# The programs of TensorE, VectorE and ScalarE written out over the batch in fourteen stages of a transformer stack

## The reference

```python
x = _layernorm(x + _L0_attn_ref(x, ...))   # causal attention, 16 heads, rotary
x = _layernorm(x + _L0_ffn_ref(x, ...))    # two layers: local rotary attention, gated feed-forward
x = _layernorm(x + _L1_attn_ref(x, ...))   # attention with a table of relative biases
x = _layernorm(x + _L1_ffn_ref(x, ...))    # projection of values rounded to a 6 bit grid, scale per 32
x = _layernorm(x + _L2_attn_ref(x, ...))   # short convolution, then running sums over time
x = _layernorm(x + _L2_ffn_ref(x, ...))    # 16 routed and 2 shared experts
x = _layernorm(x + _L3_attn_ref(x, ...))   # linear recurrence in complex numbers
x = _layernorm(x + _L3_ffn_ref(x, ...))    # as in layer 0
```

```python
# L2: the scan
phi = k_val[..., None] * theta
num_re = cumsum(p_w * cos(phi), axis=1); num_im = cumsum(p_w * sin(phi), axis=1)
out_re = sum(s_re * qr + s_im * qi, axis=-1)
...
# L1: the quantised projection
q = nearest_on_grid(blocks / scales, GRID)
out = (xq * xs) @ (wq * ws).T + bias
```

## Time and profile before

| | |
|---|---|
| time, median of 3 runs | 7667.36 us (7658.31 to 7671.06) |
| profiled execution | 7661.74 us, its span 7660.0 us |
| granted TensorE clock, mean | 0.92 |
| TensorE products busy | 6397.9 us (84%) x31876 |
| TensorE weight loads busy | 3356.0 us (44%) x31876 |
| VectorE busy | 4648.5 us (61%) x11517 |
| ScalarE busy | 2779.5 us (36%) x6066 |
| GpSimd busy | 1304.2 us (17%) x1035 |

### The profile page before, as it was taken

How to read it: one execution, slowest core, us unless ns; L and a number is a source line. 1 busy time by engine, 2 the same in 40 slices (tenths; PEclk the granted TensorE clock), 3 DMA queues, 4 the chain that set the end, 5 groups by cost and what they waited for, 6 DMA issues and landing times. The chain is left out here.

```text
span 7660.0 us, 115272 instructions
## 1 busy us (share of the span) xinstructions
PE 6397.9 (84%) x31876; PEld 3356.0 (44%) x31876; DVE 4648.5 (61%) x11517; ACT 2779.5 (36%) x6066; POOL 1304.2 (17%) x1035
## 2 busy tenths in 40 slices
PE   6788868989998966999994387986996888998979
PEld 2333334655555533333332253334554455544655
DVE  5665467733864634888875747984335765347735
ACT  0255514712462200566661104541110255224711
POOL 1101115100610003000000003550002441015100
PEclk9899979989999987999997599997998899999999
DMA  5423244542455255332323221115222355324541
GB/s 177 117 67 70 54 148 153 175 143 73 138 184 169 76 213 188 81 80 71 85 57 106 80 80 56 37 32 143 67 64 74 126 163 183 99 87 151 178 150 54
DMA packets 931136, 851.29 MB, mean 111 GB/s; under 512 B 222216, under 2 KB 785376, under 8 KB 930464
## 3 DMA queue, kind: packets, MB, share of 16 engines
q1 hardware_dynamic: 500624, 522.99, 23.8%
q10 hardware_dynamic: 430080, 323.08, 13.2%
HBM read 503.10 MB, written 346.00 MB: 111 GB/s over the span
## 5 line engine op out<-in xcount | busy, mean ns | idle before, releaser
L1267 ACT ACTIVATE Catt_E<-Catt_t 128x512 f32<-128x512 f32 x1024 | 582.5, 596 | 345.8 <-DVE Catt_t L1230 164.0
L1216 DVE CUSTOM_DVE_ANT_0 Catt_S<-Catt_s,Catt_win 128x1024 f32<-128x1024 f32 x512 | 622.7, 1218 | 90.7 <-PE Catt_s L1139 62.1
L1216 DVE CUSTOM_DVE_ANT_0 Aatt_S<-Aatt_s,Aatt_win 128x128 f32<-128x128 f32 (+7 forms) x512 | 375.6, 757 | 251.4 <-PE Aatt_s L1139 239.8
L1267 ACT ACTIVATE Aatt_E<-Aatt_t 128x512 f32<-128x512 f32 (+3 forms) x768 | 355.2, 489 | 250.2 <-PE Aatt_t L1171 171.5
L1168 PE MATMUL Catt_t<-Catt_Q,Catt_K 123*128 123x512 bf16 x1024 | 369.3, 385 | 38.4 <-ACT Catt_E L1267 17.4
L1139 PE MATMUL Catt_s<-Catt_K,Catt_Q 96*128 96x512 bf16 x1024 | 321.2, 397 | 22.2 <-DMA Catt_K<-k_parts 12.1
L1194 PE MATMUL Catt_o<-Catt_E,Catt_V 128*32 128x256 f32 x4096 | 326.5, 391 | 0.0
L2358 PE MATMUL scan_cum<-scan_X,scan_upto 128*128 128x512 f32 x512 | 265.3, 608 | 25.3 <-DVE scan_X L2427 23.9
L1168 PE MATMUL Aatt_t<-Aatt_Q,Aatt_K 99*128 99x512 bf16 (+3 forms) x768 | 241.4, 333 | 51.9 <-ACT Aatt_E L1267 27.6
L2356 PE MATMUL scan_cum<-scan_X,scan_after 128*128 128x512 f32 x448 | 239.7, 617 | 44.0 <-DVE scan_pi L2438 44.0
L1230 DVE TENSOR_TENSOR Catt_t<-Catt_t,Catt_near 128x384 f32<-128x384 f32 (+1 forms) x384 | 200.4, 522 | 116.6 <-PE Catt_t L1168 112.9
(11 more groups left out here) (723 smaller groups left out, 14584.6 us busy)
## 6 DMA issues: line engine op xcount, KB each, us to landing
moe_cb<-c_s SPq DMA_DIRECT2D x16, 1024.0 KB
bias_rows<-line SPq DMA_DIRECT2D x16, 960.0 KB, 7.1
skewed<-bias_win ACTq DMA_DIRECT2D x16, 960.0 KB
Catt_win<-skewed SPq DMA_DIRECT2D x16, 960.0 KB, 5.0
rec<-state_in_r ACTq DMA_DIRECT2D x32, 416.0 KB
scan_r<-rec SPq DMA_DIRECT2D x64, 208.0 KB, 2.5
Aatt_Q<-q_parts SPq DMA_DIRECT2D x32, 384.0 KB, 4.4
Aatt_K<-k_parts SPq DMA_DIRECT2D x32, 384.0 KB, 5.6
```

The lines of the kernel that those rows point to most:

```text
L1216: v.tensor_tensor_reduce(out=S[:, j % 2, 0:w], in0=s_ps[j % 2][:, 0:w], in1=win[:, 0 if causal else h, w0:w0 + w], scale=-1.0, scalar=BIG, ...
L1267: a.activation(E[:, kb % NB, h, lo:hi], t_ps[n % 2][:, 0:hi - lo], ACT.Exp, scale=scale).then_inc(exped, 1)
```

## The change

Fourteen calls of `pipelined` become `written_out`, and eight `Fori` loops become Python loops, on TensorE, VectorE and ScalarE of nine stage functions: `stage_project` (Eout), `stage_qkv` (Aqkv, Cqkv), `stage_local_out` (B0, B1, H0, H1), `stage_thin_out` (Aout, Cout), `stage_qkv_rotary` (four), `stage_mx_project` (Dmx), `stage_state_inputs`, `stage_state_scan` and `stage_recurrence` (lru). In these stages the three engines' programs are then straight code over all four batches. The programs of SyncE and GpSimd are as before, as are the attention stages, the gated feed-forward, the experts, the bias tables and the first stage. No instruction that computes, moves or waits is added, taken away or reordered on its engine; register and branch instructions go, and waits are for constants.

The built program goes from 18,572 to 21,183 instructions on TensorE, from 13,899 to 17,942 on VectorE and from 10,085 to 11,250 on ScalarE, since a loop's body stood there once and now stands three or four times.

```diff
@@ -427,7 +427,7 @@
                     ins = t.matmul(tail.y[s][:], aT[:, s, k * P:(k + 1) * P], w_sb[:, k, :], start=k == 0, stop=k == F - 1)
                 ins.then_inc(tail.y_done, 1)
 
-            pipelined(t, B, NT, ((0, turn_in), (1, product), (LN + 1, lambda it, u: tail.turn(t, it, u))))
+            written_out(t, B, NT, ((0, turn_in), (1, product), (LN + 1, lambda it, u: tail.turn(t, it, u))))
 
         @block.scalar
         def _(s):
...
@@ -509,7 +509,7 @@
         def _(t):
             t.sem_inc(v_done, NT)
             t.wait_ge(w_in, nw)
-            with t.Fori(0, B) as it:
+            for it in range(B):
                 for c in range(2):
                     t.wait_ge(h_in[c], it * 16 + 16)
                     for j, (m, w) in enumerate(steps):
...
@@ -904,7 +904,7 @@
         @block.vector
         def _(v):
             v.sem_inc(z_done, NT)
-            with v.Fori(0, B) as it:
+            for it in range(B):
                 for u in range(NT):
                     c, q = u // 4, u % 4
                     if q == 0:
...
@@ -1356,17 +1356,17 @@
                                    start=k == 0, stop=k == KT - 1)
                 ins.then_inc(tail.y_done, 1)
 
-            pipelined(t, B, NT, ((0, product), (LN, lambda it, u: tail.turn(t, it, u))))
+            written_out(t, B, NT, ((0, product), (LN, lambda it, u: tail.turn(t, it, u))))
 
         @block.vector
         def _(v):
             tail.prime_dve(v)
-            pipelined(v, B, NT, ((0, lambda it, u: tail.combine(v, it, u)),))
+            written_out(v, B, NT, ((0, lambda it, u: tail.combine(v, it, u)),))
 
         @block.scalar
         def _(a):
             tail.prime_act(a)
-            pipelined(a, B, NT, ((LN, lambda it, u: tail.store(a, it, u)),))
+            written_out(a, B, NT, ((LN, lambda it, u: tail.store(a, it, u)),))
             tail.finish(a)
 
 
...
@@ -2051,7 +2051,7 @@
                 for u in range(c * 4, c * 4 + 4):
                     tail.combine(v, it, u)
 
-            pipelined(v, B, 2, ((0, quantise), (1, combine)))
+            written_out(v, B, 2, ((0, quantise), (1, combine)))
 
 
 K, KQ, SH, SM = 32, 4, 8, 8
...
@@ -2446,7 +2446,7 @@
                 v.tensor_tensor(y[:, j % 2, :].rearrange("p (k h) -> p k h", k=16), ys[j % 2][:, 0:P].rearrange("p (k h) -> p k h", k=16),
                                 r[:, j % R, 3 * P + 16:].unsqueeze(2).to_broadcast([P, 16, SH]), ALU.mult).then_inc(y_done, 1)
 
-            pipelined(v, B, ST, ((1, fraction), (0, phase), (2, weigh), (3, read), (4, reduce)))
+            written_out(v, B, ST, ((1, fraction), (0, phase), (2, weigh), (3, read), (4, reduce)))
 
 
 def stage_experts(nc, act_in, router, wg, wu, wd, c_s, out):
@@ -2897,12 +2897,12 @@
                 for u in range(c * 4, c * 4 + 4):
                     tail.turn(t, it, u)
 
-            pipelined(t, B, 2, ((0, inputs), (2, turn), (1, outputs)))
+            written_out(t, B, 2, ((0, inputs), (2, turn), (1, outputs)))
 
         @block.scalar
         def _(a):
             tail.prime_act(a)
-            with a.Fori(0, B) as it:
+            for it in range(B):
                 for u in range(NT):
                     tail.store(a, it, u)
             tail.finish(a)
...
```

More of the change, by code:

```diff
@@ L442, in move_in @@
                 s.activation(aT[:, sl, :], a_ps[sl][:], act).then_inc(aT_done, 1)
-            pipelined(s, B, NT, ((0, move_in), (LN + 1, lambda it, u: tail.store(s, it, u))))
+            written_out(s, B, NT, ((0, move_in), (LN + 1, lambda it, u: tail.store(s, it, u))))
             tail.finish(s)
@@ L450, in _ @@
             combine = lambda it, u: tail.combine(v, it, u)
-            pipelined(v, B, NT, ((0, combine),))
+            written_out(v, B, NT, ((0, combine),))
 def stage_qkv(nc, name, act_in, wq, wk, wv, wqs, wks, bias, rope, q_s, k_s, v_s, scale):
@@ L1607, in turn @@
                     ins.then_inc(turned, 1)
-            pipelined(t, B, NT, ((0, products), (LAG, turn)))
+            written_out(t, B, NT, ((0, products), (LAG, turn)))
         @block.scalar
@@ L1641, in turned_out @@
                                 qo[:, o, :].rearrange("p (j t) -> p j t", j=4)).then_inc(qo_out[o], 16)
-            pipelined(a, B, NT, ((0, squares), (0, values), (LAG, turned_out)))
+            written_out(a, B, NT, ((0, squares), (0, values), (LAG, turned_out)))
             for i in range(2):
@@ L2158, in running @@
                 t.matmul(d_ps[:], upto[:], pw[:, u, :], start=u == 0, stop=True, skip_group_check=True).then_inc(den_done, 1)
-            pipelined(t, B, NT, ((0, products), (1, running)))
+            written_out(t, B, NT, ((0, products), (1, running)))
         @block.vector
@@ L2229, in weights @@
                 v.drain()
-            pipelined(v, B, NT, ((0, scores), (1, weights)))
+            written_out(v, B, NT, ((0, scores), (1, weights)))
         @block.scalar
@@ L2257, in store @@
                             ).then_inc(rec_out[m % 2], 16)
-            pipelined(a, B, NT, ((0, decayed), (1, store)))
+            written_out(a, B, NT, ((0, decayed), (1, store)))
             for i in range(2):
@@ L2391, in store @@
                             y[:, m % 2, :]).then_inc(y_out[m % 2], 16)
-            pipelined(a, B, ST, ((1, trig), (0, whole), (4, store)))
+            written_out(a, B, ST, ((1, trig), (0, whole), (4, store)))
             for i in range(2):
@@ L2938, in combine @@
                     tail.combine(v, it, u)
-            pipelined(v, B, 2, ((0, states), (1, combine)))
+            written_out(v, B, 2, ((0, states), (1, combine)))
 def bass_post_layernorm_stack(nc, ins, out):
```

## The result

The changed kernel took 7642.7 us (median of 9 runs, 7634.4 to 7646.6) against 7668.0 us (9 runs, 7658.3 to 7682.0): ratio 0.9962, 95% interval 0.9953 to 0.9971, 25 us less. The prediction said 18.4 us less (7649.0, range 7634 to 7664). The profiled execution took 7643.5 us, its span 7641.8 us.

A forecast was written before the change was run, and what follows sets the result against it. The kernel was taken as a sum of stages behind barriers, each bound by its own engine. Gains of 24.0 us less 5.6 for fetch gaps gave 18.4, from 7667.4 to 7649.0 us, range 7634 to 7664.

The forecast's parts named there:

- The price of a loop pass on VectorE: Aout, Cout, Eout, Dmx, lru, scan: VectorE's loop entries, passes and returns go, 17.5 us gained, Aout 3.0, scan 3.7.
- The fetch gaps: VectorE's longer straight code: one idle gap per 128 instructions, 32 more, 16 on the path at 0.35, 5.6 us lost.
- What a return adds before that wait is hidden by the transfer. 0.25 each, 1.0: Local outs (B0, B1, H0, H1): TensorE's wait ends with a DMA landing, which hides the return; 1.0 us gained in all.
- The same kind of cycle, 0.5: State inputs: ScalarE waits for the record's store, and register time in that cycle goes; 0.5 us gained.
- 1.0 each for Aqkv and Cqkv: VectorE waits for its own stores; part of ScalarE's and VectorE's register time is in that cycle, 2.0 us gained together.
- ScalarE as the one waited for, 3.0: TensorE waits for ScalarE's copy L282; address computations between copies go, gaining 2 us in lru and 1 in Eout.
- Rotary 0: Rotary projections: TensorE is full and VectorE's register work lies beside it, so 0 us gained.
- Busy time of every engine is unchanged: Whole kernel: a sign expected in the profile after the change, every engine's busy time as before.
- rival A: Gain swallowed by waits in Eout, Dmx, Cout and lru, with TensorE partly at its low clock: 7657.6, chance 0.35.
- Wrong would be the sum if any stage gains over 6 us (C): Any stage: a gain over 6 us was to show that each loop return is a fetch from memory.
- Rival B: Slower: fetching the straight programs costs 20 stalls of 2.5 us on VectorE, ScalarE and TensorE, 7693; chance 0.07.
- Rival C: Much larger gain: each of 18 VectorE loop returns is a memory fetch of 2.5 us, 36 more, 7613; chance 0.02.

The follow-up runs named there:

- VectorE alone: Kernel before with only VectorE's programs written out in all 17 stages, TensorE and ScalarE keeping their loops: 0.9987 of before, 10 us less.
- ScalarE alone: Kernel before with only ScalarE's programs written out in all 17 stages: 0.9983 of before, 13 us less.
- TensorE alone: Kernel before with only TensorE's programs written out in all 17 stages: 0.9999 of before.
- the path stages alone: Kernel before with all three engines written out only in Aout, Cout, Eout, Dmx, the scan and lru: 0.9981 of before, 15 us less.

## Why the prediction was right, and where its steps were wrong

The sign, the case and the size held: 25 us against 18.4. The mechanism held for VectorE's loops and for the gaps. For the rest the sum came out near through errors that offset each other: the gain in the scan's clock and most of that in the local outs weren't in it, and what it had for Eout and lru was too much. Point by point:

- **The price of a loop pass on VectorE: right.** Aout's 3.0 less four gaps of 0.35 is 1.6 (measured 2.2 as means of spans, 1.8 between the x4 rows), the scan's 3.7 was 3.3 from batch to batch. The whole agrees less well than it seems: VectorE alone gave 10 us where 17.5 less 5.6 is 11.9, but its profile has the scan 7.6 us shorter, of which some 4 are the clock, and lru at 203.8, not shorter at all, where 3.0 stood in the sum.
- **The fetch gaps: right.** 0.42 to 0.43 idle where 0.08 is usual, four in Aout, 39 packets more. They explain why Aout, the stage from which the price was read, gained less than its seven turns promised. In the scan there are none, where most instructions take 1.2 us, so the 5.6 were somewhat too much; that the longer instructions leave time to fetch is my reading. The Trainium skill ("Runtime: NRT & Kernel Launch", Instruction fetch mechanics) has fetching mostly hidden: the scan agrees, the rows at 1012.04 and 1034.55 don't. The 7643 that the prediction gave for this rule is what was measured, 7642.7, but by luck: the gaps are there and paid for.
- **"What a return adds before that wait is hidden by the transfer. 0.25 each, 1.0": wrong.** The local outs gave 6.6. TensorE's long wait of 18.8 us at the start is the transfer's and stayed. But the three later ones ended with a transfer that itself came sooner, 6.0 us after its issue instead of 6.6. I looked at what the waiting engine's own loop adds, not at the engine whose store was issued in the same moment as the load.
- **"The same kind of cycle, 0.5" for the state inputs, and 1.0 each for Aqkv and Cqkv: too small.** 3.4, 1.8 and 2.0. ScalarE alone gave 242.8 us in the state inputs, against 250.3, but TensorE alone gave 245.8, which no cycle through ScalarE's store explains. If each of 32 tiles paid 0.1 us of issue time, that would be 3.2; this is an estimate that no run tests, and the cause stays open.
- **ScalarE as the one waited for, 3.0: the wait fell, the span not by as much.** TensorE waits for L282 in lru 14 times, 10.0 us, instead of 16 times, 12.6, in every profile in which ScalarE is straight there. But with ScalarE alone its wait for VectorE at L208 was 7.8 us instead of 4.5, and lru took 201.6, no less than the 201.0 of the second profile of before. What ends last there is in part VectorE. ScalarE as a whole was worth 13 us; its profile has 7 of them in the local outs and as much in the state inputs.
- **Rotary 0: nearly.** +2.6, and not within 0.5 us each: B0qkv took 223.5 instead of 221.5. VectorE's extra program brings nothing there. Its busy time rose instead, by an instruction of 32 columns that now takes longer. From the page grouped by line, VectorE in B0qkv before:

```profile
L1674 DVE TENSOR_SCALAR B0qkv_ss<-B0qkv_ss 128x32 f32<-128x32 f32 x16 | 16.5, 1033 | 0.0
```

and in the changed kernel:

```profile
L1674 DVE TENSOR_SCALAR B0qkv_ss<-B0qkv_ss 128x32 f32<-128x32 f32 x16 | 20.0, 1247 | 0.0
```

  In the same view the idle time ahead of L1660 fell from 6.2 to 2.4 us, so time moved from one line to the other and VectorE gained nothing.

- **"Busy time of every engine is unchanged": wrong.** The clock was missing from the sum, in both directions, and the rival A had it as a loss only. In the scan it is shown (7 to 15 us in the long tiles, see above). For the rest of TensorE's 13.7 us it is not: in lru its busy time was 121.85 us and 117.21 in two executions of the kernel before, with spans of 204.5 and 201.0, so half of the 6.8 us between the profiles of before and after is no gain of the change.
- **"Wrong would be the sum if any stage gains over 6 us (C)": three did** in the profile of the changed kernel, the scan 7.8, lru 6.8 and moe 8.9. It is not C, as no return costs more than the rows have it. The sign was badly chosen: the falls of the clock move a stage by several us on their own.
- The scan's sum has three returns of 0.45; the rows show two tiles of 7.87 and 7.83, and one of 7.53 at the entry. The low end's 25.5 leaves out the upper bounds of Aqkv and Cqkv, 2.8 more. Neither decides anything.
- Rival A didn't come: Dmx, Eout, Cout and lru gained 9.8 us together by the table, where A was to show under 4. Rival B, dear fetching, didn't either: no gap without a releaser above 0.5 us in Aout. Rival C neither: VectorE's returns cost what the earlier trace rows show.

What stays open: what decides whether the clock falls after an idle time of 3.7 us, since 3.71 brought a fall at four places of the changed kernel and none at three, and 3.75 a fall at one place of the kernel before and none at another; whether its four places instead of six come from the straight code or from chance, since the path stages alone had six with the same tiles; how much of lru's 3.8 us is ScalarE and how much the clock; and what shortens the state inputs.

## What to carry to other kernels

A loop that stands beside its own first pass in straight code is a measurement of what unrolling gives; read it turn by turn, and take off one fetch gap of 0.4 us per 128 VectorE instructions of short work, drains and waits counted. Ask also for the engines that only start transfers: 0.14 us less between an addition and its store went with a load landing 0.6 us sooner that is issued in the same moment, and with 1.6 us less per stage. Below 0.5% a change moves stages that it doesn't touch, so compare stage spans over several profiles before explaining one.

## What the runs showed of the hardware

- VectorE's straight code idles 0.42 to 0.43 us every 128 instructions of short work (drains and semaphore waits counted, rows at 1012.04 and 1034.55), and not visibly in the scan, where most instructions take 1.2 us.
- A load of 1024 KB and a store of 512 KB start together in the local outs. With the store 0.19 us ahead they land 6.0 and 4.4 us after their issue, with the store 0.04 us ahead 6.6 and 7.2.
- After an idle time of 3.7 us TensorE's granted clock is 0.50, 1.2 GHz, at some places (a pair of products takes 2.08 us instead of 1.02) and 1.00 at others. Products with zero weights in that idle time left no long tile after the first five in three profiles, and made the scan 8.8 us shorter in the kernel before.
- 101 DRAIN instructions on VectorE ahead of moe took its first turn from 61.3 to 59.3 us; 130 left it at 61.3.
